# Vision tower on one core: the class token's mixed row, the last group's statistics, and the first stores of the convolution's output

## The reference, cut to what matters

```python
h = tok(x)                    # 64 images: 196 patches of 16x16 through rfft2 and a projection to 192
                              # channels, a class token in front: (64, 197, 192), plus positions
h = h + attn(layernorm(h))    # per channel a causal convolution over the 197 tokens with kernel K[d, :]
h = h + ffn(layernorm(h))     # a shared expert and 2 of 8 routed experts for each token
return h
```

## Time and profile before

| | |
|---|---|
| median of 3 runs | 1213.37 us (1209.41 to 1216.26) |
| profiled execution | 1206.76 us |
| its span | 1204.9 us |
| mean granted TensorE clock | 0.951 |
| PE, DVE, ACT, POOL busy | 88%, 75%, 47%, 55% |
| `embed` ends, `mix` starts | 226.9 us |
| `mix` ends, `feed_forward` starts | 308.8 us |

### The profile page before, as it was taken

How to read it: one execution, slowest core, us unless ns; L and a number is a source line. 1 busy time by engine, 2 the same in 40 slices (tenths; PEclk the granted TensorE clock), 3 DMA queues, 4 the chain that set the end, 5 groups by cost and what they waited for, 6 DMA issues and landing times. The chain is left out here.

```text
span 1204.9 us, 25722 instructions
## 1 busy us (share of the span) xinstructions
PE 1056.5 (88%) x8503; PEld 751.5 (62%) x8504; DVE 902.1 (75%) x2723; ACT 562.1 (47%) x1076; POOL 658.8 (55%) x680
## 2 busy tenths in 40 slices
PE   5978999487089999899999999599999999984997
PEld 4968889476046666565666666366666666652555
DVE  6999866222368879798888877478888888872998
ACT  1143543222355556556555554166566566651332
POOL 0124422000147778777777786048888788874553
PEclk9989899798599999999999999899999999996999
DMA  8686686988888434354344311634444454434997
GB/s 310 215 281 218 233 281 168 233 164 194 187 183 197 126 102 130 101 138 123 96 101 107 95 55 59 199 108 126 139 145 132 128 145 144 137 105 148 296 301 244
DMA packets 213445, 198.55 MB, mean 165 GB/s; under 512 B 69864, under 2 KB 192266, under 8 KB 213062
## 3 DMA queue, kind: packets, MB, share of 16 engines
q1 hardware_dynamic: 178624, 144.84, 43.6%
q0 software_dynamic: 19488, 39.17, 9.6%
q10 hardware_dynamic: 15206, 12.93, 4.1%
HBM read 123.59 MB, written 74.41 MB: 164 GB/s over the span
## 5 line engine op out<-in xcount | busy, mean ns | idle before, releaser
L1698 POOL DMA_INDIRECT parts<-unit_yu,unit_token x208 | 225.0, 1082 | 59.8 <-issue 59.2
L1261 POOL DMA_INDIRECT routed<-rows_w,slot x198 | 217.5, 1099 | 64.8 <-issue 64.8
L1111 PE MATMUL pso<-ffn_w_hi,hh 128*128 128x192 f16 x480 | 118.9, 248 | 21.4 <-DVE hl L1448 16.5
L1443 DVE SCALAR_TENSOR_TENSOR hf<-psu,sg 128x512 f32<-128x512 f32 x120 | 82.8, 690 | 70.6 <-PE psu L1096 42.6
L1184 ACT ACTIVATE sg<-psg 128x512 f32<-128x512 f32 x120 | 71.9, 599 | 128.8 <-PE psg L1096 128.8
L420 POOL TENSOR_TENSOR e_rs<-e_ve,mhalf 98x8 f32<-98x8 f32 x16 | 49.8, 3112 | 144.3 <-DVE e_ve L648 144.3
L1111 PE MATMUL pso<-ffn_w_hi,hl 128*128 128x192 f16 x480 | 118.9, 248 | 0.0
L1111 PE MATMUL pso<-ffn_w_lo,hh 128*128 128x192 f16 x480 | 118.8, 247 | 0.0
L1096 PE MATMUL psg<-xt,ffn_w_hi 128*128 128x512 f16 x360 | 118.1, 382 | 0.0
L1096 PE MATMUL psu<-xt,ffn_w_hi 128*128 128x512 f16 x360 | 117.2, 380 | 0.0
L480 PE MATMUL ps<-w,area 128*98 128x192 f32 x528 | 99.9, 333 | 0.0
(11 more groups left out here) (247 smaller groups left out, 2971.0 us busy)
## 6 DMA issues: line engine op xcount, KB each, us to landing
unit_xu<-routed SPq DMA_DIRECT2D x53, 392.0 KB
end_part<-parts SPq DMA_DIRECT2D x48, 384.0 KB, 5.6
area<-in_xa_dram SPq DMA_DIRECT2D x33, 392.0 KB, 5.2
area<-in_xb_dram SPq DMA_DIRECT2D x33, 392.0 KB, 6.4
resid<-spare ACTq DMA_DIRECT2D x32, 294.0 KB
hin<-resid SPq DMA_DIRECT2D x24, 384.0 KB
yin<-mixed SPq DMA_DIRECT2D x96, 96.0 KB
area<-taps SPq DMA_DIRECT2D x12, 600.2 KB
```

Source lines behind the costliest of these rows:

```text
L1111: last = nc.tensor.matmul(o, hx[m % 2][:, ts], wd[k][:, m], start=(a == 0 and m == 0 and t % 2 == 0), stop=(a == 2 and m == NSH - 1), skip ...
L1261: nc.gpsimd.indirect_dma_start(out=routed[:, :], out_offset=bass.IndirectOffsetOnAxis(ap=slot[q][:, k, t:t + 1], axis=0), in_=rows_w[q][:, ...
L1443: nc.vector.scalar_tensor_tensor(out=hf[i][:], in0=psu[:, i], scalar=1.0 / SCALE, in1=sg[i][:], op0=ALU.mult, op1=ALU.mult).then_inc(s["hf ...
L1698: nc.gpsimd.indirect_dma_start(out=parts[:, :], out_offset=bass.IndirectOffsetOnAxis(ap=token[q][:, k:k + 1], axis=0), in_=y[q][:, k, :], ...
```

## The change

1. The four DMAs that write `yc` leave the end of `embed`. DVE makes `yc` in `mix`, before its eviction of step 12, and SP writes it after the loads of the weights, and waits for it at the end of `mix`. `uc`, `k0` and `yc` live in both blocks.
2. In the last group of `embed` DVE takes the statistics of a tile right after its eviction.
3. `store_mixed` can cut the 196 patches of its images into pieces, one DMA for each piece. Images 0 to 2 of `area` go out in 4 pieces, that is 8 DMAs of three images instead of 2.
4. Images 3 to 15 of `area` are stored by SP in `shared_expert`, behind the loads of block 0 and ahead of weight pieces 2 and 3.

```diff
@@ embed, ACT
-            act.wait_ge(s["uc_ready"], 2)
-            for c in range(4):
-                act.dma_start(mixed[c].rearrange("(b l) d -> l b d", l=SEQ)[0:1],
-                              yc[0:1, c * DQ:(c + 1) * DQ].unsqueeze(1).to_broadcast([1, B, DQ])
-                              ).then_inc(row_out, 16)
@@ embed, DVE
+            def statistics(g, m):
+                name, count = evictions(g, m)
+                dve.wait_ge(s[name], count)
+                if m == 0:
+                    dve.wait_ge(s["mv_ready"], g)
+                for k in range(2):
+                    last = nc.vector.bn_stats(st[:, 2 * m + k], h[g % NH][:, m, k])
+                return last
...
+                    if g == NG - 1:
+                        last = statistics(g, m)
...
-                for n in range(2 * GI):
-                    last = nc.vector.bn_stats(st[:, n], h[i][:, n // 2, n % 2])
+                for m in range(GI if g < NG - 1 else 0):
+                    for k in range(2):
+                        last = nc.vector.bn_stats(st[:, 2 * m + k], h[i][:, m, k])
...
-            dve.wait_ge(s["k0_in"], 64)
-            dve.wait_ge(s["uc_ready"], 1)
-            nc.vector.scalar_tensor_tensor(out=yc[:], in0=k0[:], scalar=1.0 / SCALE, in1=uc[0:1, :],
-                                           op0=ALU.mult, op1=ALU.mult).then_inc(s["uc_ready"], 1)
@@
-def store_mixed(queue, y, mixed, n, done, first, last):
+def store_mixed(queue, y, mixed, n, done, first, last, pieces=1):
     for q in range(2):
-        rows = mixed[2 * n + q].rearrange("(b l) d -> b (l d)", l=SEQ)[first:last, DQ:SEQ * DQ]
-        queue.dma_start(rows, y[q * B + first:q * B + last].rearrange("p l d -> p (l d)")).then_inc(done, 16)
+        rows = mixed[2 * n + q].rearrange("(b l) d -> b l d", l=SEQ)[first:last, 1:SEQ]
+        for l in range(0, NPATCH, NPATCH // pieces):
+            part = slice(l, l + NPATCH // pieces)
+            queue.dma_start(rows[:, part].rearrange("b l d -> b (l d)"),
+                            y[q * B + first:q * B + last, part].rearrange("p l d -> p (l d)")).then_inc(done, 16)
@@ mix, SP, behind load_weights
+            sp.wait_ge(yc_ready, 1)
+            for c in range(4):
+                sp.dma_start(mixed[c].rearrange("(b l) d -> l b d", l=SEQ)[0:1],
+                             row["yc"][0:1, c * DQ:(c + 1) * DQ].unsqueeze(1).to_broadcast([1, B, DQ])
+                             ).then_inc(row_out, 16)
             sp.wait_ge(row_out, 16 * 4)
@@ mix, ACT
-            store_mixed(act, y[1], mixed, 1, block_stored, 0, BLOCK_IMAGES)
-            store_mixed(act, y[1], mixed, 1, y_stored, BLOCK_IMAGES, FIRST_IMAGES)
+            store_mixed(act, y[1], mixed, 1, block_stored, 0, BLOCK_IMAGES, PIECES)
@@ mix, DVE
+                if n == HG:
+                    dve.wait_ge(row["in"], 64)
+                    nc.vector.scalar_tensor_tensor(out=row["yc"][:], in0=row["k0"][:], scalar=1.0 / SCALE,
+                                                   in1=row["uc"][0:1, :], op0=ALU.mult, op1=ALU.mult
+                                                   ).then_inc(yc_ready, 1)
@@ shared_expert, SP
-            sp.wait_ge(block_stored, 64)
+            sp.wait_ge(block_stored, 32 * (1 + PIECES))
             load(0, 0, NT)
+            store_rest(1, area, y_stored, BLOCK_IMAGES, FIRST_IMAGES)
             stage_in(2)
             stage_in(3)
             sp.wait_ge(y_stored, 32)
             load(1, 1, NT)
```

More of the change, by code:

```diff
@@ L66 @@
 BLOCK_IMAGES = -(-BT // SEQ)
+PIECES = 4
 NSH = HS // 128
@@ L193, in load_toeplitz, with embed @@
                     bass.AP(taps.tensor, n * (CG * RW) + SKIP, [(RW * D, 1), (RW, CG), (1, TC)])).then_inc(landed, 16)
-def embed(nc, io, u, area, taps, resid, mixed, consts, early_in, row_out, yc, spare, weights):
+def embed(nc, io, u, area, taps, resid, mixed, consts, early_in, row, spare, weights):
     with ExitStack() as ctx:
@@ L227, in embed @@
         crs = sb("crs", [3, 1])
-        uc = sb("uc", [3, D])
-        k0 = sb("k0", [1, D])
+        uc, k0 = row["uc"], row["k0"]
         xa, xb = pixel_slots(area, spare)
@@ L255, in embed @@
                  "cmv_ready", "cve_ready", "uc_ready", "vector_done", "powers_ready",
-                 "kf_ready", "taps_out", "taps_rest", "k0_in", "out_done",
+                 "kf_ready", "taps_out", "taps_rest", "out_done",
                  "folded", "eh_ready", "es_ready", "tokens_ready", "h_act", "h_dve", "stats_ready", "mv_ready", "ve_ready", "rs_ready", "nb_ready",
@@ L330, in taps_first @@
                             act.dma_start(dst.rearrange("p (g c) -> p g c", c=CG // 2),
-                                         rows[q:q + 1]).then_inc(s["k0_in"], 16)
+                                         rows[q:q + 1]).then_inc(row["in"], 16)
             def rest_high(m):
@@ L702, in _, with mix @@
             last.then_inc(s["u_ready"], 1)
-            dve.wait_ge(s["k0_in"], 64)
-            dve.wait_ge(s["uc_ready"], 1)
-            nc.vector.scalar_tensor_tensor(out=yc[:], in0=k0[:], scalar=1.0 / SCALE, in1=uc[0:1, :],
-                                           op0=ALU.mult, op1=ALU.mult).then_inc(s["uc_ready"], 1)
-def store_mixed(queue, y, mixed, n, done, first, last):
-    for q in range(2):
-        rows = mixed[2 * n + q].rearrange("(b l) d -> b (l d)", l=SEQ)[first:last, DQ:SEQ * DQ]
-        queue.dma_start(rows, y[q * B + first:q * B + last].rearrange("p l d -> p (l d)")).then_inc(done, 16)
-def mix(nc, u, area, y_stored, taps, mixed, early_in, row_out, spare, block_stored, io, weights):
+def store_mixed(queue, y, mixed, n, done, first, last, pieces=1):
+    for q in range(2):
+        rows = mixed[2 * n + q].rearrange("(b l) d -> b l d", l=SEQ)[first:last, 1:SEQ]
[3 more added lines that the diff above has]
+                            y[q * B + first:q * B + last, part].rearrange("p l d -> p (l d)")).then_inc(done, 16)
+def mix(nc, u, area, taps, mixed, early_in, row, spare, block_stored, io, weights):
     with ExitStack() as ctx:
@@ L732, in mix @@
         t_in = [sem(f"t_in{i}") for i in range(NTAP)]
-        conv0, conv1, y0, y1 = (sem(n) for n in ("conv0", "conv1", "y0", "y1"))
+        conv0, conv1, y0, y1, yc_ready, row_out = (sem(n) for n in ("conv0", "conv1", "y0", "y1", "yc_ready", "row_out"))
         block = ctx.enter_context(nc.Block())
@@ L1011, in stage_in, with store_rest @@
                 load_weights(sp, io, weights, n)
-            sp.wait_ge(block_stored, 64)
+            def store_rest(n, x, done, first, last):
+                y = x[:, 0:NPATCH * DQ].rearrange("p (l d) -> p l d", l=NPATCH)
+                store_mixed(sp, y, mixed, n, done, first, last)
+            sp.wait_ge(block_stored, 32 * (1 + PIECES))
             load(0, 0, NT)
+            store_rest(1, area, y_stored, BLOCK_IMAGES, FIRST_IMAGES)
             stage_in(2)
@@ L1018, in _ @@
             load(1, 1, NT)
-            def store_rest(n, x, done, first, last):
-                y = x[:, 0:NPATCH * DQ].rearrange("p (l d) -> p l d", l=NPATCH)
-                store_mixed(sp, y, mixed, n, s[done], first, last)
             cut = (FIRST_IMAGES + B) // 2
-            store_rest(0, spare, "spare_out", FIRST_IMAGES, B)
+            store_rest(0, spare, s["spare_out"], FIRST_IMAGES, B)
             for b in range(NBLK - 2):
@@ L1031, in _ @@
                 if b == 1:
-                    store_rest(1, area, "area_out", FIRST_IMAGES, cut)
+                    store_rest(1, area, s["area_out"], FIRST_IMAGES, cut)
                 if b == 2:
-                    store_rest(1, area, "area_out", cut, B)
+                    store_rest(1, area, s["area_out"], cut, B)
                 if staged_at(b + 1):
@@ L1976, in build @@
         block_stored = outer.enter_context(nc.semaphore("block_stored"))
-        row_out = outer.enter_context(nc.semaphore("row_out"))
         early_in = [outer.enter_context(nc.semaphore(f"early_in{i}")) for i in range(NEARLY)]
@@ L1981, in build @@
             u = ctx.enter_context(nc.sbuf_tensor("u", [128, 2, B, D], F32))
-            yc = ctx.enter_context(nc.sbuf_tensor("yc", [1, D], F32))
-            embed(nc, io, u, area, taps, resid, mixed, consts, early_in, row_out, yc, spare, weights)
-            mix(nc, u, area, y_stored, taps, mixed, early_in, row_out, spare, block_stored, io, weights)
+            row = {name: ctx.enter_context(nc.sbuf_tensor(name, [n, D], F32)) for name, n in (("uc", 3), ("k0", 1), ("yc", 1))}
+            row["in"] = ctx.enter_context(nc.semaphore("k0_in"))
+            embed(nc, io, u, area, taps, resid, mixed, consts, early_in, row, spare, weights)
+            mix(nc, u, area, taps, mixed, early_in, row, spare, block_stored, io, weights)
         feed_forward(nc, io, spare, area, block_stored, y_stored, weights, resid, mixed, routed, parts, out, consts)
```

## The result

The changed kernel takes 1219.93 us (median of 5 runs, 1218.67 to 1223.75); the kernel before took 1212.46 us in 5 runs beside it (1209.41 to 1216.26). The ratio is 1.0079, with a 95% interval of 1.0053 to 1.0106: slower, by just over the 0.5% that can be told from no change. The predicted time of 1218.5 us is 1.4 us off, and the range held it. The forecast difference was 5.1 us; between the medians it is 7.5 us. The profiled execution took 1218.87 us (span 1217.0) against 1206.76 us, 12.1 us more. The execution profiled before lay 5.7 us under its median and this one 1.1 us under its own, so 4.6 us of the 12.1 belong to the two executions and not to the change. The steps are read from these two traces one by one, with that in mind.

What follows compares the result with a forecast made beforehand. PE, 88% busy and hardly stopping from 345 us, bounds the kernel, so delays before that reach the end. -0.4 - 0.5 - 2.0 + 8.0 = +5.1 us on the median 1213.4 gave 1218.5 us; 8-in-10 range 1209 to 1223.

Steps and rivals of the forecast that it cites:

- row leaves `embed`: Joint `embed` to `mix`: SP starts about 2.9 us earlier, but step 6's tile stands behind a full DMA; 0.4 us gained.
- statistics tile by tile: End of `embed`: six of eight `bn_stats` come 1.6 us earlier, hidden under SP's issues; worth 0.
- pieces: Joint `mix` to `shared_expert`: images 0 to 2 land in 7.9 us without big stores beside them; 0.5 us gained.
- load 0, images 3 to 15 on SP: Start of `shared_expert`: load 0's issues gain 2.0 us; the store ahead of weights and load 2 costs 8.0 us in SP's queue.
- at the sum of block 2: DVE's sum in `shared_expert`, taken at load 2's landing: the terms add to +5.1 us, all reaching the end.
- The upper bound of 7 us: Issue time of the eight small stores: 2 us, or up to 7 if held like the last big one, 2.25.
- the halves run one behind the other: Rival on SP's store of images 3 to 15: 11.4 us instead of 8.0, giving +8.5, 1221.9 us; chance 0.18.
- Where the stall goes: Start of `shared_expert`: from POOL to the weights' DMA; piece 2 at 326.4, normalization at 327.5, DVE waits 3.8 us for load 2.
- load 0 at 310.7: Sign that the forecast is right: SP's load 0 at about 310.7 us.
- the end of `mix` under 1 us earlier: Sign that the forecast is right: `mix` ends under 1 us earlier than before.
- DVE's wait until 356: Sign in the shared expert that the forecast is right: DVE waits for load 2 until about 356 us.
- within 0.5%: Class of no tellable change against the kernel before, 0.5% being 6.1 us; chance 0.61.

Runs made afterwards that it cites:

- row_only: The kernel before with only the class token's row made in `mix` and stored by SP; 1.0000 of the kernel before.
- tile_order_before: The kernel before with only the order of toeplitz tiles in `mix` changed: step 12 first, then 6 to 11, then 13 to 15; 1203.11 us, 0.9938.
- row_stats: The kernel before with the row moved to `mix` and the last group's statistics taken tile by tile, stores as before; 1209.05 us, 0.9990.
- row_order_stats: row_order with the last group's statistics taken tile by tile as well; 1203.34 us, 0.9922 of the kernel before.
- one_piece: The changed kernel with images 0 to 2 stored uncut (PIECES 1 instead of 4), images 3 to 15 still on SP; 1.0077 of the kernel before.
- Weights_first: The changed kernel with SP's store of images 3 to 15 behind weight pieces 2 and 3 instead of ahead; 1.0028 of the kernel before.
- row_order: row_only with toeplitz tile 12 loaded first, then 6 to 11, then 13 to 15; 1202.5 us, 0.9910 of the kernel before.
- act_stores: The changed kernel with images 3 to 15 stored by ACT again, behind the pieces; 1.0056 of the kernel before.

## Why the prediction was right, and where it was not

| step | forecast, us | measured, us | shown by |
| --- | --- | --- | --- |
| row leaves `embed` | -0.4 | 0 in the traces | row_only, tile_order_before |
| statistics tile by tile | 0 | 0 in the times | row_stats, row_order_stats |
| pieces | -0.5 | +0.8 | after, one_piece |
| load 0, images 3 to 15 on SP | -2.0 + 8.0 | +6.1 | interval 45.9 against 39.8 |
| end of `mix` | not in the sum | +1.9 | after; cause open |
| at the sum of block 2 | +5.1 | +8.8 | |

**The row leaves `embed`:** right, with the reason, as far as the traces go. PE's wait at step 6 was forecast at 5.7 us and is 6.36, and the tile lands 0.2 us sooner than before. The experiments add what the prediction did not see: it is the order of the tiles that makes PE wait, and that was worth 7.3 us by itself (1203.11 against 1210.38 us, tile_order_before; 5.2 us at the sum of block 2 in the trace).

**Statistics:** right in the times, nothing. Whether they move the end of `mix` is open, see below.

**Pieces:** this is the term with the wrong sign. I took 0.5 us for the absence of the big stores beside the block's. One_piece shows that their absence is worth nothing: 8.43 us in one piece alone, 8.37 us before. Cutting costs: 9.14, 9.21 and 9.13 us in the three kernels with eight small stores. That cutting along the patches spreads nothing held; the eight issues themselves took 6.21 us and ended ahead of the landing. The upper bound of 7 us that was given for them does not follow from the row that it names, eight times 2.25 us being 18. The Trainium skill's rule that was set beside this term (DMA: Bandwidth & Descriptors, section "Why a DMA increments its semaphore by 16 and not by 1") gives three engines for three rows, cut or not; the runs agree in that the landing did not become shorter, and none of them shows what a real spread would give.

**Load 0 and the queue:** these two terms gave +6.0, and the three kernels with the store on SP show +6.1, +6.0 and +5.9 (45.88, 45.74 and 45.68 against 39.75). That the sum came out so well is in part luck. Taken apart along SP's queue, from the start of load 0 to the sum of block 2: load 0's issues take 2.83 us instead of 5.05 (-2.2, forecast -2.0); from there to the start of load 1 it takes 10.81 us instead of 1.29 (+9.5, forecast 8.0); load 1's issues take 3.33 us instead of 4.77 (-1.4, not in the sum); the rest, from the store of 48 images on, 28.91 instead of 28.64 us (+0.3). The price of the store was taken 1.5 us too low, and a gain of load 1 that the sum did not hold made up for most of it. The way is another one in part, too. I had the price as bytes ahead in SP's queue. It is a wait: SP stops ahead of load 1 until `y_stored` is complete, 10.8 us after it issued the store, so that load 0 and load 1 start 13.6 us apart instead of 6.3. Weights_first shows it: with the weights out of the way the same landing ends the same wait. So the rival "the halves run one behind the other" had more of the truth in it than I gave it: 10.4 to 10.8 us are close to its 11.4, and 1.3 of them SP needed for the weights' issues anyway.

**Where the stall goes:** right in direction. ACT waits for piece 2 (forecast 326.4, measured 329.23), not for POOL; its normalization was forecast at 327.5 and starts at 330.22; and DVE's wait for load 2 was forecast at 3.8 us and is 4.83. Of the signs that were named, the start of `mix` (223.6), the pairs of `bn_stats` and piece 2 came as forecast; load 0 at 310.7 (measured 314.30), the end of `mix` under 1 us earlier (1.9 later) and DVE's wait until 356 (360.2) did not.

**What the sum left out.** At the sum of block 2, 3.7 us are missing. Of these 1.3 are the pieces, 0.4 the row, 0.1 load 0 and the queue, and 1.9 the later end of `mix`. For that last one I have no cause. With the old order of tiles `mix` ends at 301.99 to 303.35 in the four kernels without the second part of the change and at 303.44 to 306.62 in the five with it, so the statistics are the suspect. Against them stands that row_stats is no slower than the kernel before (0.9990, at most 1.0004), and that with the new order of tiles row_order_stats ends `mix` 0.5 us ahead of row_order. With one trace of each kernel, and that of row_stats 6.8 us above its median, it stays open. Behind the sum of block 2 come 1.4 us from the lower clock after PE's pause, which the prediction did not have: it took a delay to be handed on one to one. One_piece, with a pause of 3.35 us there and a clock of 1.00, shows that they are not paid every time. Some 2 us more come in the last third of the program; no run here tells them from the spread of single executions.

**The chances.** The likeliest class was "within 0.5%", with 0.61. The measured 0.79% lies beyond it, in the class that had 0.31. With the pieces at their measured size (1.3 us more) the forecast would have been 6.4 us, just beyond the bound of 6.1. That the time of 1218.5 us was met to 1.4 us is partly luck: the difference was 2.4 us short, and the median of the kernel before, on which the forecast stood, fell by 0.9 us with the further runs.

## What to carry to other kernels

Moving a DMA to another queue moves its completion too, and a consumer's wait on that queue then stands behind it in order: ask which wait on the new queue names this very transfer, and price the landing, not the bytes. A wait that a profile shows on an engine (3 us of SP at the joint) was worth nothing here, since the resource behind it (the DMA engines, 0.99 busy) is what the next consumer waits for; in such a place it is the order of what is queued that can be gained, here 0.6% by the order of the tiles alone. And small stores in front of a large one on the same queue can delay the large one into whatever comes next, even if they carry the same bytes: here load 0 took 8.81 us to issue instead of 4.57. A clock that drops behind a pause in one execution is no price of the change before a second execution shows it.

## What the runs showed of the hardware

- Six rows of 36.8 KB (three images in two halves) in two DMAs land in 8.4 us, beside 0.96 MB of other stores (before: 8.37) or alone (8.43). In eight DMAs of a quarter of their length they need 9.1 to 9.2 us. In six DMAs of one row they need 9.8 us.
- A DMA of one row written as sixteen adjacent parts still went out in large packets, 31 packets for 0.83 MB in that stretch.
- The time that an issue takes on its engine depends on what is in flight: two weight issues took 1.23 us before and 7.22 us behind the store of images 3 to 15 on the same queue; the four issues of `yin` for block 0 took 2.34 us without ACT's large stores beside them (after), 4.57 us beside their tail (before) and 8.81 us where those stores start later (act_stores).
- The pause of 3.51 us on PE was followed by 6 us at a granted clock of 0.76. Pauses of 3.35 us (one_piece) and 1.11 us (before) at the same product were followed by a clock of 1.00. At an earlier product, 3.57 us (before) was followed by 1.00 and 3.64 us (row_only) by 0.72.
